# A recommender forward pass on one core: bottom parts placed ahead of the last gathered lots of the first chunk, and unread matmuls beside two waits

## The chip, the cores and the metric

The kernel runs on one core of a Trainium2 chip. The metric is the time of one execution on the device in microseconds; the median of several executions is given. The core has five engines with a queue of instructions each: TensorE (PE, matmuls and transposes), VectorE (DVE), ScalarE (ACT), GpSimd (POOL, here the gathers) and SyncE (SP, here the plain DMAs). Engines wait for one another on semaphores. What TensorE writes goes to PSUM, in banks of 512 float32 columns; everything else lies in SBUF, or in DRAM.

## What is computed

A batch of 512 samples has 13 dense numbers and 26 table indices each.

```python
def mlp(x, Ws, bs):
    for W, b in zip(Ws, bs):
        x = relu(x @ W + b)
    return x
bot_out = mlp(dense_x, [bw0, bw1, bw2], ...)              # 13 -> 512 -> 256 -> 128
gathered = stack([emb[t][sparse_x[:, t]] for t in range(26)], axis=1)
features = concatenate([bot_out[:, None, :], gathered], axis=1)   # 27 features of 128
Z = einsum('bnd,bmd->bnm', features, features)
interact = Z[:, LI, LJ]                                   # the 351 pairs i > j
x = concatenate([bot_out, interact], axis=1)              # 479
return mlp(x, [tw0, tw1, tw2, tw3, tw4], ...)             # 1024, 1024, 512, 256, 1
```

## The kernel before

The batch is cut into four chunks of 128 samples, a chunk into two halves of 64. The order on every engine is written out by hand; nothing reorders it. The chunks are software-pipelined: while TensorE does the top layers of chunk c, it also does the transposes and pair products of chunk c+1.

**Gathers.** GpSimd issues 26 indirect DMAs for each chunk, 13 for each half, in lots of 4, 4, 4 and 1. Each brings 128 rows of an embedding table. `pace` holds some of them back with waits on events of TensorE. In the fill (the gathers numbered up to 35), gather 31 waits for the second pair products of chunk 0 (`s_z` at 2). In chunk 0's stage, gather 37 waits until the first lot of chunk 1 is turned, and gather 39 for the end of layer 0's first half (`s_l[0]`).

**Features.** `turn_lot(c, h, j)` (L755) transposes a lot on TensorE into bank j of the tensor `feat`. `feature_lot` copies it from there into `featT`: ScalarE takes lots 0 and 2, VectorE lots 1 and 3. `dots_of(c, h)` waits for both copies and does the pair products of a half, 32 small matmuls in the program, 64 in the trace (L781). They are written into `feat` again. `dots_out` copies them out on ScalarE and VectorE into `dots`, SyncE writes them to a scratch in DRAM and reads them back with the pairs on the partitions, in three tiles (`pairs`). ScalarE rounds each tile to `xh` (L464), VectorE makes the rest `xl`.

**Top layers.** Layer 0 has two halves of 512 columns in the banks `acc0` and `acc1`, and three pair tiles. Each product is three matmuls (`product`, L799, L800 and L803): high part by high weight, high by low, low by high. The part of layer 0 that comes from the bottom output is worked out ahead: for chunk 0 into `acc0` and `acc1` directly, right behind the second pair products; for chunks 1 to 3 as six parts g = 0 to 5 (`bot_parts`), into the banks `turned0` (even g) and `turned1` (odd g) in turn. A part may be written when the copy of the part before it in the same bank is done; `bot_part_out` (L243) makes those copies, parts 0, 2, 4 and 5 on ScalarE (`s_prea`), 1 and 3 on VectorE (`s_pred`). They are read in chunks 1 to 3.

**Weights.** Each large weight arrives in pieces. ScalarE rounds a piece to its high part (L439), TensorE brings that into `acc0` and `acc1` by a product with the identity (`hi_back`, L823), and VectorE subtracts it from the raw weight (L595) to get the low part; `s_wl` counts these halves. Pieces 0 to 9 go that way; the last two of the group are subtracted without TensorE (L600).

"The regroup" is the stretch between the second pair products of chunk 0 and its layer 0, in which the pairs go through DRAM. Behind it SyncE issues the loads of w2, w3 and the top rows.

Of the kernel before, what the change touches and what calls it, by code (L numbers as in the profile page):

```python
# [23 lines left out]
P = 128  # L24
# [24 lines left out]
NB = 512  # L49
# [45 lines left out]
def after(eng, sem, count):  # L95

    if count > 0:
        eng.wait_ge(sem, count)


def rec_kernel(nc, x_turned, sparse, emb, bw, small, w0_bot, w0_pairs, w1, w2, w3_in, top_rows, scratch, out):
    with ExitStack() as ctx:
        def sb(name, shape, dt=F32, scope=ctx):
            return scope.enter_context(nc.sbuf_tensor(name, shape, dt))
# [53 lines left out]
        with ExitStack() as early:  # L158
            wbh = sb("wbh", [P, T0], F32R, early)
# [14 lines left out]
        def banks(name, n=1):  # L174
            return ctx.enter_context(nc.psum_tensor(name, [P, n * NB], F32))[:]

        acc = [banks("acc0"), banks("acc1")]
        turned = [banks("turned0"), banks("turned1")]
# [3 lines left out]
        def feat_bank(j):  # L182
            return feat[:, j * NB:(j + 1) * NB]

        def acc_of(c, half):
            return acc[half]
# [8 lines left out]
        s_wh, s_wb, s_wl, s_identr = map(sem, ("weight_hi", "weight_hi_in_psum", "weight_lo_halves", "ident_rounded"))  # L195
# [8 lines left out]
        s_bh, s_bl, s_pre, s_prea, s_pred = map(  # L204
            sem, ("bot_hi", "bot_lo", "bot_part_done", "bot_part_copied_act", "bot_part_copied_dve"))
# [24 lines left out]
        NEAR = UPPER - 2  # L230
# [7 lines left out]
        PARTS = 2 * (CHUNKS - 1)  # L238
        part_banks = [turned[g % 2] for g in range(PARTS)]

        def bot_part_out(eng, copy, g, done):
            eng.wait_ge(s_pre, g + 1)
            copy(bot_part[:, g // 2, g % 2 * NB:(g % 2 + 1) * NB], part_banks[g]).then_inc(done, 1)  # L243
# [7 lines left out]
        def lot_size(j):  # L251
            return min(LOT, GATHERS - LOT * j)

        def lot_out(h, j):
            n = PER_GATHER * lot_size(j)
            at = 1 + PER_GATHER * LOT * j
            return (featT[:, h, :, at:at + n].rearrange("d b n -> d n b"),
                    feat_bank(j)[:, 0:n * HALF].rearrange("d (n b) -> d n b", b=HALF))
# [172 lines left out]
        def _(act):  # L431
# [3 lines left out]
            def weight_hi(n):  # L435

                raw, hi, _ = pieces[n]
                act.wait_ge(s_piece[n], 16)
                nc.scalar.copy(hi, raw).then_inc(s_wh, 1)  # L439

            def feature_lot(c, h, j):

                act.wait_ge(s_ft, LOTS * (HALVES * c + h) + j + 1)
                nc.scalar.copy(*lot_out(h, j)).then_inc(s_fa, 1)  # L444

            def dots_out(c, h):

                after(act, s_scr0[h], 16 * c)
                after(act, s_scr1[h], 16 * c)
                act.wait_ge(s_z, HALVES * c + h + 1)  # L450
                nc.scalar.copy(*dot_quadrant(h, 0))
                nc.scalar.copy(*dot_quadrant(h, 1)).then_inc(s_za, 1)
# [62 lines left out]
            weight_hi(9)  # L515
            bot_part_out(act, nc.scalar.copy, 2, s_prea)
            weight_hi(NEAR)
            feature_lot(0, 1, 2)
            for g in range(PARTS - 2, PARTS):
                bot_part_out(act, nc.scalar.copy, g, s_prea)  # L520
            dots_out(0, 1)
            weight_hi(NEAR + 1)

# [230 lines left out]
        def _(pe):  # L754
            def turn_lot(c, h, j):  # L755

                half = HALVES * c + h
                pe.wait_ge(s_gather[LOTS * h + j], 16 * lot_size(j) * (c + 1))
                if j == 0:
                    after(pe, s_za, half)  # L760
                    after(pe, s_zd, half)
                for i in range(lot_size(j)):
                    ins = nc.tensor.transpose(feat_bank(j)[:, i * P:(i + 1) * P],  # L763
                                              rows[:, h * GATHERS + LOT * j + i, :], ident[:])
                ins.then_inc(s_ft, 1)

            def dots_of(c, h):

                half = HALVES * c + h
                pe.wait_ge(s_fa, 2 * half + 2)  # L770
                pe.wait_ge(s_fd, 2 * half + 2)
                pe.wait_ge(s_fb, half + 1)
                (sample_pairs if half < HALVES * CHUNKS - 1 else single_samples)(h)
# [23 lines left out]
            def product(dst, ah, al, wh, wl, first, end, lo_ready=None):  # L797

                nc.tensor.matmul(dst, ah, wh, start=first, stop=False)  # L799
                nc.tensor.matmul(dst, ah, wl, start=False, stop=False)  # L800
                if lo_ready is not None:
                    pe.wait_ge(*lo_ready)
                return nc.tensor.matmul(dst, al, wh, start=False, stop=end)  # L803

            def bot_times_w0(dst, c, half):

                at, cols = slice(c * P, (c + 1) * P), slice(half * NB, (half + 1) * NB)
                return product(dst[:], botTh[:, at], botTl[:, at], wbh[:, cols], wbl[:, cols], True, c > 0)

            def bot_parts(gs):  # L810
                for g in gs:
                    after(pe, s_pred if g % 2 else s_prea, g // 2)
                    bot_times_w0(part_banks[g], g // 2 + 1, g % 2).then_inc(s_pre, 1)

            def hi_back(n):

                if n == 0:
                    pe.wait_ge(s_identr, 1)
                    pe.wait_ge(s_h0, 2)
                pe.wait_ge(s_wh, n + 1)  # L820
                for x in range(2):
                    after(pe, s_wl, 2 * (n - 1) + x + 1)
                    nc.tensor.matmul(acc[x], ident_r, pieces[n][1][:, x * NB:(x + 1) * NB],  # L823
                                     start=True, stop=True).then_inc(s_wb, 1)
# [106 lines left out]
            for o in range(B0 // P):  # L931
                nc.tensor.matmul(bottom_banks[o][:], v0[:, o * P:(o + 1) * P], x0T[:], start=True,
                                 stop=True).then_inc(s_l0b, 1)
            pe.wait_ge(s_v[1], 16)
            for k in range(B0 // P):
                pe.wait_ge(s_h0, k + 1)
                for o in range(B1 // P):
                    ins = nc.tensor.matmul(turned[o][:], v1[:, k, o * P:(o + 1) * P], h0T[:, k, :],
                                           start=(k == 0), stop=(k == B0 // P - 1))
                    if k == B0 // P - 1:  # L940
                        ins.then_inc(s_l1b, 1)
                if k < 3:
                    hi_back(k)
                if k == 1:
                    pe.wait_ge(s_h0, B0 // P)
                    turn_lot(0, 0, 0)
            turn_lot(0, 0, 1)
            hi_back(3)
            pe.wait_ge(s_v[2], 16)
            for k in range(B1 // P):  # L950
                pe.wait_ge(s_h1, k + 1)
                ins = nc.tensor.matmul(turned[0][:], v2[:, k, :], h1T[:, k, :], start=(k == 0),
                                       stop=(k == B1 // P - 1))
            ins.then_inc(s_l2b, 1)
            hi_back(4)
            turn_lot(0, 0, 2)
            turn_lot(0, 0, 3)
# [10 lines left out]
            hi_back(8)  # L968
            bot_parts(range(2, 4))
            hi_back(9)  # L970
            turn_lot(0, 1, 2)
            turn_lot(0, 1, 3)
            bot_parts(range(4, 6))
            dots_of(0, 1)
            for half in range(2):
                pe.wait_ge(s_wl, 2 * (NEAR - 1) + half + 1)
                bot_times_w0(acc_of(0, half), 0, half)
            turn_lot(1, 0, 0)

            def chunk(c):  # L980
# [100 lines left out]
```

## Time and profile before

| | us |
|---|---|
| median of 3 runs | 182.41 |
| lowest and highest of them | 181.74, 182.44 |
| the profiled execution | 183.45 |
| its span, first to last instruction | 181.5 |
| TensorE busy in it | 166.4 |
| GpSimd busy in it | 100.7 |
| VectorE, ScalarE busy | 82.0, 66.6 |

The profiled execution lies above the three runs; the profile's times are on its own span, from 0 to 181.5 us. A row of the timeline gives start, length, engine, line, operation, what is written from what, and in brackets the idle time ahead of it with what ended it. Matmuls are pipelined: their lengths overlap, so the distance of two starts tells how fast they go. In the slices of the page each digit is the busy share of a fortieth of the span (4.54 us).

### The profile page before, as it was taken

To read this page: it belongs to the slowest core of one execution; us is meant where nothing else is said; L and a number is where in the kernel's file an instruction comes from. 1 tells how busy PE (TensorE), PEld (TensorE's weight loads), DVE (VectorE), ACT (ScalarE), POOL (GpSimd) and SP (SyncE) were. 2 spreads that over 40 slices of the span, in tenths; PEclk is the share of its full clock that TensorE was granted. 3 is DMA by queue.
4 is the path that set the end of the run, shared out by engine and by line. 5 is a ranking of instruction groups with operands and counts; after the bars stand their busy time and mean duration, and the time that the engine had idled before them with its cause. 6 is when DMAs were issued, how large, how long until landed. Compare 5 with 4: busy or idle time off the path is not lost.

```text
span 181.5 us, 3287 instructions
## 1 busy us (share of the span) xinstructions
PE 166.4 (92%) x1340; PEld 128.3 (71%) x1340; DVE 82.0 (45%) x177; ACT 66.6 (37%) x103; POOL 100.7 (55%) x112
## 2 busy tenths in 40 slices
PE   2999999779099999998999999999999999999993
PEld 1435557448066888797878889977887897788892
DVE  4204498924217557773443246253515625411422
ACT  0576858635031637432034253212514512110201
POOL 4777777776766777777777777777772000000000
PEclk9999999978958999999999999999999999999999
DMA  4989973322589924342222245322223120000000
GB/s 100 350 327 385 386 264 77 89 46 50 108 263 311 376 60 87 73 100 66 58 50 55 56 95 94 84 54 62 44 58 72 23 48 12 4 0 0 0 0 0
DMA packets 10122, 19.91 MB, mean 110 GB/s; under 512 B 5638, under 2 KB 5770, under 8 KB 9980
## 3 DMA queue, kind: packets, MB, share of 16 engines
q1 hardware_dynamic: 6636, 12.89, 22.1%
q0 software_dynamic: 3328, 6.82, 16.7%
q8 instruction: 10, 0.16, 0.4%
q14 instruction: 4, 0.03, 0.1%
q10 hardware_dynamic: 144, 0.00, 0.0%
HBM read 18.26 MB, written 1.44 MB: 109 GB/s over the span
## 4 chain that ended last, share of the span: by engine, by line
PE 42%; POOL 29%; DMA 12%; issue 12%; DVE 2%; SPq 1%; ACT 1%; POOLq 0%; DVEq 0%; ACTq 0%
POOL rows L420 29%; PE acc L799 10%; PE acc L803 9%; PE acc L800 9%; DMA rows<-in_emb,index 5%; PE feat L781 5%; DMA pairs<-pair_scratch 3%; DMA pair_scratch<-dots 3%; PE turned L875 2%; PE feat L763 2%; DMA index_raw<-in_sparse 1%; PE feat L793 1%; PE turned L889 1%; DVE dots L622 1%; DVE dots L621 1%
## 5 line engine op out<-in xcount | busy, mean ns | idle before, releaser
L420 POOL DMA_INDIRECT rows<-in_emb,index x104 | 99.5, 956 | 35.6 <-issue 30.3
L799 PE MATMUL acc<-w1h,y_split 128*128 128x512 f32 x64 | 27.4, 428 | 0.0
L803 PE MATMUL acc<-w1h,y_split 128*128 128x512 f32 x64 | 25.6, 400 | 0.0
L800 PE MATMUL acc<-w1l,y_split 128*128 128x512 f32 x64 | 25.2, 393 | 0.0
L457 ACT ACTIVATE y_split<-turned 128x512 fp32r<-128x512 f32 x16 | 9.7, 609 | 36.4 <-PE turned L875 36.4
L444 ACT COPY featT<-feat 128x512 f32<-128x512 f32 x16 | 17.5, 1093 | 12.9 <-PE feat L763 12.8
L651 DVE SCALAR_TENSOR_TENSOR y_split<-turned,y_split 128x512 fp32r<-128x512 f32 x16 | 11.1, 692 | 19.1 <-ACT y_split L457 19.0
L799 PE MATMUL acc<-w2h,y_split 128*128 128x256 f32 x64 | 18.9, 295 | 0.0
L763 PE MATMUL feat<-ident,rows 128*128 128x128 f32 x104 | 15.2, 275 | 3.2 <-DMA rows<-in_emb,index 3.2
L803 PE MATMUL acc<-w2h,y_split 128*128 128x256 f32 x64 | 18.0, 282 | 0.0
L800 PE MATMUL acc<-w2l,y_split 128*128 128x256 f32 x64 | 17.9, 280 | 0.0
L763 PEld LDWEIGHTS feat<-ident,rows 128*128 128x128 f32 x104 | 12.2, 140 | 7.2 <-DMA rows<-in_emb,index 4.6
L799 PE MATMUL acc<-w0h,xh 117*128 117x512 f32 (+1 forms) x24 | 12.2, 508 | 5.3 <-ACT xh L464 5.3
L781 PEld LDWEIGHTS feat<-featT 128*59 128x59 f32 x448 | 13.5, 141 | 2.9 <-issue 2.1
L607 DVE COPY featT<-feat 128x512 f32<-128x512 f32 (+1 forms) x16 | 11.8, 741 | 8.2 <-PE feat L763 8.2
L803 PEld LDWEIGHTS acc<-w1h,y_split 128*128 128x128 f32 x64 | 12.0, 188 | 4.3 <-DVE y_split L651 1.7
L781 PE MATMUL feat<-featT 128*59 128x54 f32 x448 | 14.4, 225 | 0.1
L799 PEld LDWEIGHTS acc<-w1h,y_split 128*128 128x128 f32 x64 | 12.2, 190 | 3.1 <-ACT y_split L457 1.4
L621 DVE COPY dots<-feat 27x416 f32<-27x416 f32 x8 | 4.7, 587 | 20.2 <-PE feat L781 19.5
L800 PEld LDWEIGHTS acc<-w1l,y_split 128*128 128x128 f32 x64 | 12.1, 189 | 1.7
L799 PEld LDWEIGHTS acc<-w2h,y_split 128*128 128x128 f32 x64 | 12.0, 188 | 0.2
L800 PEld LDWEIGHTS acc<-w2l,y_split 128*128 128x128 f32 x64 | 12.0, 188 | 0.0
(103 smaller groups left out, 253.9 us busy)
## 6 DMA issues: line engine op xcount, KB each, us to landing
w1r<-in_w SPq DMA_DIRECT2D x8, 512.0 KB, 15.1
w2r<-in_w SPq DMA_DIRECT2D x4, 512.0 KB, 6.1
rows<-in_emb,index POOLq DMA_INDIRECT x104, 3.1
w0r<-in_w_pairs SPq DMA_DIRECT2D x3, 512.0 KB, 8.8
top<-in_top_rows SPq DMA_DIRECT2D x1, 1024.0 KB, 11.6
pair_scratch<-dots SPq DMA_DIRECT2D x8, 104.0 KB, 2.4
pair_scratch<-dots SPq DMA_DIRECT2D x8, 71.5 KB
v<-in_bw SPq DMA_DIRECT2D x1, 512.0 KB, 3.7
```

The costliest lines, as they stand in the source:

```text
L420: pool.indirect_dma_start(rows[:, i, :], None, table, bass.IndirectOffsetOnAxis(ap=index[:, c, i:i + 1], axis=0)).then_inc(s_gather[LOTS * ...
L444: nc.scalar.copy(*lot_out(h, j)).then_inc(s_fa, 1)
L457: nc.scalar.activation(yh[:, half, :], turned[half][:], ACT.Relu).then_inc(s_yh[layer], 1)
L607: nc.vector.tensor_copy(*lot_out(h, j)).then_inc(s_fd, 1)
L621: nc.vector.tensor_copy(*dot_quadrant(h, 2))
L651: nc.vector.scalar_tensor_tensor(out=yl[:, half, :], in0=turned[half][:], scalar=0.0, in1=yh[:, half, :].bitcast(F32), op0=ALU.max, op1=AL ...
L763: ins = nc.tensor.transpose(feat_bank(j)[:, i * P:(i + 1) * P], rows[:, h * GATHERS + LOT * j + i, :], ident[:])
L781: ins = nc.tensor.matmul(feat[QUAD * q:QUAD * q + PAIR_COLS, at:at + 2 * FEATS].rearrange("n (s m) -> n s m", s=2), samples.rearrange("d s ...
L799: nc.tensor.matmul(dst, ah, wh, start=first, stop=False)
L800: nc.tensor.matmul(dst, ah, wl, start=False, stop=False)
L803: return nc.tensor.matmul(dst, al, wh, start=False, stop=end)
L875: ins = nc.tensor.transpose(turned[half][:, i * P:(i + 1) * P], y_evac[:, half, i * P:(i + 1) * P], ident[:])
```

## The change

On TensorE, bottom parts 4 and 5 are put ahead of the transposes of the last two lots of chunk 0 instead of behind them. Ahead of the second pair products come three matmuls of 512 columns into `acc0` whose result nobody reads, behind a wait on the weight difference that last read that bank. Between the bottom products of chunk 0 and the transposes of chunk 1's first lot come eleven such matmuls into `turned0`, behind a wait for three copies of parts on ScalarE. On ScalarE the copy of part 4 goes ahead of the copy of lot 2.

```diff
@@ scalar
             weight_hi(NEAR)
+            bot_part_out(act, nc.scalar.copy, PARTS - 2, s_prea)
             feature_lot(0, 1, 2)
-            for g in range(PARTS - 2, PARTS):
-                bot_part_out(act, nc.scalar.copy, g, s_prea)
+            bot_part_out(act, nc.scalar.copy, PARTS - 1, s_prea)
             dots_out(0, 1)
             weight_hi(NEAR + 1)
@@ tensor
+            def keep_going(bank, times):
+                for _ in range(times):
+                    nc.tensor.matmul(bank[:], wbh[:, 0:P], wbh[:, 0:NB], start=True, stop=True)
@@ tensor
             hi_back(9)
+            bot_parts(range(4, 6))
             turn_lot(0, 1, 2)
             turn_lot(0, 1, 3)
-            bot_parts(range(4, 6))
+            pe.wait_ge(s_wl, 2 * (NEAR - 1) + 1)
+            keep_going(acc[0], 3)
             dots_of(0, 1)
             for half in range(2):
                 pe.wait_ge(s_wl, 2 * (NEAR - 1) + half + 1)
                 bot_times_w0(acc_of(0, half), 0, half)
+            pe.wait_ge(s_prea, PARTS // 2)
+            keep_going(turned[0], 11)
             turn_lot(1, 0, 0)
```

How it stands on the engines. TensorE around the last two lots of chunk 0, before: the transposes (L763), then part 4 (`turned0`) and part 5 (`turned1`), then the pair products (L781).

```order
50 L823 MATMUL acc1<-w1h,xl 128x512
51 L763 MATMUL feat<-ident,rows 128x128 x5
52 L799 MATMUL turned0<-wbh,botTh 128x512
53 L800 MATMUL turned0<-wbl,botTh 128x512
54 L803 MATMUL turned0<-wbh,botTl 128x512
55 L799 MATMUL turned1<-wbh,botTh 128x512
56 L800 MATMUL turned1<-wbl,botTh 128x512
57 L803 MATMUL turned1<-wbh,botTl 128x512
58 L781 MATMUL feat<-featT 59x54 x32
```

The same place of TensorE in the changed kernel (L829 is the line that was L823, L819 the unread matmul).

```order
50 L829 MATMUL acc1<-w1h,xl 128x512
51 L799 MATMUL turned0<-wbh,botTh 128x512
52 L800 MATMUL turned0<-wbl,botTh 128x512
53 L803 MATMUL turned0<-wbh,botTl 128x512
54 L799 MATMUL turned1<-wbh,botTh 128x512
55 L800 MATMUL turned1<-wbl,botTh 128x512
56 L803 MATMUL turned1<-wbh,botTl 128x512
57 L763 MATMUL feat<-ident,rows 128x128 x5
58 L819 MATMUL acc0<-wbh 128x512 x3
59 L781 MATMUL feat<-featT 59x54 x32
```

The two parts stand ahead of the five transposes, and three unread matmuls between these and the products.

ScalarE at the same place, the difference (L444 is the copy of lot 2).

```order
 L439 CAST w1h<-w1r 128x1024
+L243 COPY bot_part<-turned0 128x512
 L444 COPY featT<-feat 128x8x64
-L243 COPY bot_part<-turned0 128x512
 L243 COPY bot_part<-turned1 128x512
 L451 COPY dots<-feat 27x26x16
```

The copy of part 4 has moved ahead of the lot copy; that of part 5 has stayed.

TensorE in the regroup of the changed kernel, between the last bottom product of chunk 0 and layer 0 (before, L763 stands directly behind L803).

```order
65 L803 MATMUL acc1<-wbh,botTl 128x512
66 L819 MATMUL turned0<-wbh 128x512 x11
67 L763 MATMUL feat<-ident,rows 128x128 x4
68 L799 MATMUL acc0<-w0h,xh 128x512
69 L800 MATMUL acc0<-w0l,xh 128x512
```

Eleven unread matmuls stand ahead of the transposes of chunk 1's first lot. The orders of VectorE, GpSimd and SyncE are the same.

## Rows read from the trace of the kernel before

**Rows 1.** The page: span, TensorE's slices, and the clock row.

```profile
span 181.5 us, 3287 instructions
...
PE   2999999779099999998999999999999999999993
...
PEclk9999999978958999999999999999999999999999
```

**Rows 2.** The chain that ended last: start us, us, what was worked on.

```profile
39.90 0.43 PE turned L800
...
70.77 2.93 DMA rows<-in_emb,index
...
74.31 0.23 PE acc L800
...
112.23 0.95 POOL rows L420
```

**Rows 3.** Timeline of TensorE's matmuls: start us, us, engine, line, operation, count [idle before].

```profile
26.56 1.94 PE L781 MATMUL feat<-featT 128*59 128x54 f32 x64
...
32.36 0.66 PE L763 MATMUL feat<-ident,rows 128*128 128x128 f32 x4 [0.68 <-DMA rows<-in_emb,index]
...
34.90 0.92 PE L823 MATMUL acc<-w1h,xl 128*128 128x512 f32 x2
37.34 0.66 PE L763 MATMUL feat<-ident,rows 128*128 128x128 f32 x4 [1.52 <-DMA rows<-in_emb,index]
38.29 0.33 PE L763 MATMUL feat<-ident,rows 128*128 128x128 f32 x1 [0.29 <-DMA rows<-in_emb,index]
...
40.68 2.72 PE L781 MATMUL feat<-featT 128*59 128x54 f32 x64
...
44.84 0.60 PE L763 MATMUL feat<-ident,rows 128*128 128x128 f32 x4
49.76 0.79 PE L799 MATMUL acc<-w0h,xh 117*128 117x512 f32 x1 [4.32 <-ACT xh L464]
...
52.88 0.79 PE L799 MATMUL acc<-w0h,xh 118*128 118x512 f32 x1 [0.20 <-ACT xh L464]
...
73.75 0.33 PE L763 MATMUL feat<-ident,rows 128*128 128x128 f32 x1 [0.43 <-DMA rows<-in_emb,index]
```

**Rows 4.** Timeline of ScalarE, 34 to 50 us.

```profile
34.42 0.59 ACT L243 COPY bot_part<-turned 128x512 f32<-128x512 f32 x1 [1.39 <-PE turned L803]
...
38.03 1.07 ACT L444 COPY featT<-feat 128x512 f32<-128x512 f32 x1 [2.08 <-PE feat L763]
...
49.41 0.30 ACT L464 CAST xh<-pairs 118x128 fp32r<-118x128 f32 x1 [3.88 <-DMA pairs<-pair_scratch]
```

**Rows 5.** Timeline of VectorE, 35 to 44 us.

```profile
35.18 0.68 DVE L243 COPY bot_part<-turned 128x512 f32<-128x512 f32 x1
35.78 1.27 DVE L595 TENSOR_TENSOR w1l<-w1r,acc 128x512 fp32r<-128x512 f32 x2
...
43.45 0.59 DVE L621 COPY dots<-feat 27x416 f32<-27x416 f32 x1 [4.40 <-PE feat L781]
```

**Rows 6.** Timeline of GpSimd: the gathers around the two waits.

```profile
43.69 0.94 POOL L420 DMA_INDIRECT rows<-in_emb,index  x1 [1.04 <-PE feat L781]
...
52.47 0.95 POOL L420 DMA_INDIRECT rows<-in_emb,index  x1 [0.30 <-issue]
55.33 1.08 POOL L420 DMA_INDIRECT rows<-in_emb,index  x1 [1.91 <-PE acc L803]
```

**Rows 7.** Windows of 1 us: stretch, length, busy us by engine, granted clock, DMA share, GB/s.

```profile
39.00:40.00 1.00, 1.00 (x4) 0.81 (x3) 0.06 (x1) 0.60 (x2) 0.78 (x1) 0.50 0.27 62
42.00:43.00 1.00, 1.00 (x36) 1.00 (x34) 0.00 (x0) 0.00 (x0) 0.65 (x1) 0.80 0.33 66
...
49.00:50.00 1.00, 0.24 (x1) 0.24 (x2) 0.26 (x1) 0.30 (x1) 0.70 (x2) 0.62 0.40 96
...
56.00:57.00 1.00, 1.00 (x8) 0.83 (x7) 0.59 (x2) 0.00 (x0) 0.70 (x2) 0.97 1.11 352
```

## Prediction

> **What bounds the kernel now.** I read the page's own slices first, then the chain of work that ended last, then the timelines of the five engines from 34 to 60 us, and last the windows that give TensorE's granted clock.
>
> The page shows TensorE busy in nines almost everywhere; the thin places after the fill are slices 8 to 13, and the clock row dips in the same ones [rows 1]. So a gain there counts only if the work behind it can start earlier too.
>
> The chain says what that work is. Over the last gathered rows, the bottom parts (in which a matmul of 0.43 us stands on it), the second pair products, the copies and the scratch round trip it comes to layer 0, and from the end of layer 0's first half it goes back to GpSimd, whose gathers carry it from 55.33 to the landing of chunk 1's last row block at 73.70 (70.77 and 2.93); TensorE carries it on to 112.23, where gathers take it again [rows 2, 6]. There is one chain with two runners: TensorE and the gather engine. TensorE reached the last block of chunk 1 only 0.43 us before it landed [rows 3].
>
> In TensorE's timeline the reader is to see four things. After the weight products with the identity end at 35.82 it idles until 37.34, and again 0.29 before 38.29 [rows 3]. Then it runs the six matmuls of parts 4 and 5 before the products, which start at 40.68 although the ScalarE copy of lot 2, their last input, was over at 39.10 [rows 3, 4]. Then the products take 2.72 us where the same 64 took 1.94 in the first half [rows 3]. Last, after the regroup's transposes it idles 4.32 us until layer 0 at 49.76 [rows 3].
>
> The clock explains the lengths. It is low (1.2 GHz) by 39.0, since the stretch from 39 to 40 has 0.50 throughout; it is full (2.4 GHz) again at about 42.4 (0.80 over 42 to 43), low at about 49.2 (0.62 over 49 to 50), and full from about 56.1 (0.97 over 56 to 57) [rows 7]. A 512-column matmul starts every 0.43 us at the low level and every 0.23 at the full one [rows 2].
>
> **Part 1: parts 4 and 5 ahead of the last two lots.** They need copies of parts 2 and 3, done at 35.01 on ScalarE and 35.86 on VectorE [rows 4, 5]. Part 4 can follow at once at 35.65, part 5 at about 36.3: six matmuls at 0.23 are 1.4 us and end near 37.1, in the idle stretch before 37.34. So they cost nothing there; at the low level they would take 2.6 and hold the last lots up by about 0.9. The clock is full there, so I take nothing. On ScalarE the copy of part 4 now stands ahead of the copy of lot 2, and behind that one stands lot 2's semaphore for the products. Part 4 is finished near 36.5, a copy is 0.59, so it is over by 37.1 and the lot copy still starts at 38.03 [rows 4]. The copy of part 5 stays behind the lot copy and ends near 39.7, before the products are over. VectorE, SyncE and GpSimd keep their order.
>
> The products' start moves from 40.68 to 39.15, 0.05 behind the lot copy (39.10): **1.53 us**.
>
> **Part 2: 3 unread matmuls ahead of the products.** They wait for the first half of the weight difference that VectorE began at 35.78 and ended (both halves) by 37.05 [rows 5], so for nothing. The last transpose starts at 38.29; three at 0.23 fill 38.4 to 39.1, when TensorE would wait for the lot copy. Cost nothing at the full level, and up to 0.5 at the low one. With the 1.5 us hole and this one filled, what went ahead of the fall at 39.0 is gone, and the products run at the full level: 1.94 and not 2.72, which is **0.78 us**. Sum: the products end at 41.1, not 43.4, **2.3 us** earlier.
>
> **Part 3: what hangs on the products.** Copies out, scratch write and read are fixed steps: 43.45 on VectorE to 49.41 (first pair tile on ScalarE) is 5.96 [rows 4, 5]. So xh comes at 47.1, layer 0 at 47.45 and not 49.76, its third tile's matmuls at 50.58 and not 52.88 [rows 3].
>
> **Part 4: 11 unread matmuls in the regroup.** They wait for three ScalarE copies of parts (0, 2 and 4), long done. The six bottom products for chunk 0 run 41.1 to 42.5, then 11 at 0.23, 2.5 us, to about 45.1, then the four transposes, to 45.7. Layer 0 is due at 47.45, so they cost nothing: slack 1.7 us. They leave two idle stretches, 45.7 to 47.45 and (its six first matmuls take 1.4) 48.9 to 50.58. Moved behind them are those transposes (44.84 before, 45.1 now), whose copy on ScalarE comes only behind the third pair tile; the gather that waits for them would start at 50.5. Nothing is late.
>
> Is the clock still full for layer 0? Unseen in this trace; I bound it. If full throughout: before, from 52.88 to 56.1 TensorE worked at half rate, 1.6 us lost, all of it regained. If low until the very same moment 56.1: 50.58 to 56.1 at half rate loses 2.8, that is 1.2 more than before. The idle that went ahead of the first fall was 1.5 plus 0.3 us with transposes between [rows 3], and 1.75 plus 1.7 is no less, so I lean to a low stretch that remains. TensorE's own gain at 56 us is then between 1.1 (2.3 less 1.2) and 3.9 (2.3 plus 1.6).
>
> **Part 5: the gather engine caps it.** One gather waits for the products: it starts at 43.69 with the one before done at 42.65; with the usual 0.30 it starts at 42.95 [rows 6], 0.74 earlier. The seven up to the one at 52.47 follow at the same pace: the last of them starts at 51.73 and is done at 52.68. The next waits for layer 0's first half, 2.45 behind the third tile's first matmul (52.88 to 55.33), so 53.03 with 50.58; GpSimd itself is free at 52.98. So 55.33 becomes 53.0: **2.3 us**, and by no clock more. The twelve gathers behind it, to the one that leaves at 70.77, are 1.28 apart on average and wait for none of the events that TensorE would now reach later than they do, so the last block lands at 71.4. TensorE, with a gain of 1.1 to 3.9 and its 0.43 of idle, is there 1.5 to 4.3 earlier. What counts is the smaller: **1.5 to 2.35**. Behind it all moves alike: the same round trip for chunk 1, the gathers at 112.23 released by TensorE.
>
> Sum against the profiled execution: 183.45 (span 181.5 and 1.95 around it), less 1.5 to 2.35, is 181.1 to 181.95. It stands 1.04 over the median of 182.41, and I carry the difference over: 180.06 to 180.9. The three runs differ by 0.70, so before itself does not always lose the same to the clock; that, too, speaks for less than the cap. I take 1.9: **180.5**.
>
> **A rule that speaks against it.** The rows: the clock fell at 39.0 after a stretch in which near half of TensorE's busy time was transposes [rows 3, 7]. The Trainium skill, TensorE: Matmul & The Clock Gate, Part 4: PE-mode transpose, says that transposes don't count as TensorE activity the way matmuls do. By that the two lots at 37.34 and 38.29 stay a hole for the clock in spite of parts and fillers around them; by the row alone it is the idle that matters, and that is gone. The trace agrees with either.
>
> **The rivals.**
> Rival 1, the clock falls near 39 all the same: for it, 1.0 us of transposes and 0.5 of idle remain there; against it, a 0.68 us wait at 32.36, between dense work, was followed by no fall [rows 3, 7]. The 2.72 us of before held 1.7 at the low level and 1.0 at the full; with 1.94 for all at the full one, all at the low one would be 3.6. Started at 39.3 and low until 42.4 they end at 42.7, 0.7 earlier. Time 181.7.
> Rival 2, the round trip gives it back: it now runs beside other gathers, with w2's loads queued right behind it. If the 5.96 us become 8, only 0.3 is left: 182.1. Against it: the loads shift along, and the gathers beside it are as many as before.
> Rival 3, slower: the low level lasts from 39.0 through the regroup. Fillers to 39.8, products to 43.4 (3.6 us, the end of before), six matmuls to 46.0, 11 fillers of 0.43 to 50.7, transposes to 51.6, layer 0's first six to 54.2; the third tile began at 52.88 before. That is 1.3 later: 183.7. It decides where the regroup's fillers outlast the round trip: 1.7 us of slack against 2.2 of extra filler time alone. Against it: in before the level rose at 42.4 under dense work.
> That fillers are not issued is excluded: the order has both groups, 3 and 11.
>
> **How the numbers follow.** Forecast 0.76 (179.9 to 181.0), rival 1 0.11, rival 2 0.09, rival 3 0.04. The range for 8 in 10 runs from 179.8, a little under the cap, to 181.8, which takes in rival 1. A measurement here tells 0.5%, 0.9 us, from no change: faster 0.78 (the forecast and the good edge of rival 1, 0.02), same 0.17, slower 0.05.
>
> **What would show it.** In the changed profile: parts 4 and 5 at 35.6 to 37.1; products near 39.2, 1.9 long, with the clock full from 38 to 43; the 11 at 42.5 to 45.1; layer 0 at about 47.5; the gather of 55.33 at 53.0 with about 0.3 idle before it; TensorE waiting longer than 0.43 for the last block of chunk 1 near 71.4. It is wrong if the products take over 2.5 us (rival 1), if 5.96 us from the products to xh grows (rival 2), if layer 0 finds xh waiting (rival 3), or if a wait further on takes the lead, such as the w2 and w3 loads.

## The result, and the profile after

| | before | changed |
|---|---|---|
| median of 20 runs, us | 182.7 | 181.2 |
| lowest, us | 180.56 | 180.47 |
| profiled execution, us | 183.45 | 181.54 |
| its span, us | 181.5 | 179.6 |
| mean granted clock in it | 0.972 | 0.991 |

The ratio of the changed kernel to before is 0.9933, with an interval from 0.9912 to 0.9954: faster by 0.5 to 0.9 per cent, about 1.2 us. Every ratio here is taken over the fast runs alone, without those more than 1.5 per cent above the fastest of their kernel, and every median over all runs. The forecast was 180.5 and a gain of 1.9. The two profiled executions differ by exactly that, 1.9; the medians by 1.5.

The page of the changed kernel, against [rows 1]: the clock dips of slices 9 to 13 are gone, and one stands further on.

```profile
span 179.6 us, 3315 instructions
...
PE   1999999899599994999999999989999999999993
...
PEclk9999999999999999799999999999999999999999
```

TensorE's timeline of the changed kernel, against [rows 3] (start us, us, engine, line, operation, count, idle before):

```profile
36.41 0.39 PE L799 MATMUL turned<-wbh,botTh 128*128 128x512 f32 x1
...
37.79 0.60 PE L763 MATMUL feat<-ident,rows 128*128 128x128 f32 x4
38.61 0.33 PE L763 MATMUL feat<-ident,rows 128*128 128x128 f32 x1 [0.22 <-DMA rows<-in_emb,index]
38.69 0.95 PE L819 MATMUL acc<-wbh 128*128 128x512 f32 x3
39.57 1.94 PE L781 MATMUL feat<-featT 128*59 128x54 f32 x64
...
42.94 2.66 PE L819 MATMUL turned<-wbh 128*128 128x512 f32 x11
45.43 0.60 PE L763 MATMUL feat<-ident,rows 128*128 128x128 f32 x4
47.97 0.50 PE L799 MATMUL acc<-w0h,xh 117*128 117x512 f32 x1 [1.94 <-ACT xh L464]
...
50.01 0.40 PE L799 MATMUL acc<-w0h,xh 118*128 118x512 f32 x1
...
70.37 0.65 PE L763 MATMUL feat<-ident,rows 128*128 128x128 f32 x4 [1.81 <-DMA rows<-in_emb,index]
71.69 0.48 PE L763 MATMUL feat<-ident,rows 128*128 128x128 f32 x1 [0.67 <-DMA rows<-in_emb,index]
...
74.63 1.95 PE L781 MATMUL feat<-featT 128*59 128x54 f32 x64
```

Parts 4 and 5 lie ahead of the lots, the products start right behind the three unread matmuls and take 1.94 us, layer 0 starts 1.8 us earlier than at 49.76. And then TensorE waits 1.81 and 0.67 us for the last two lots of chunk 1, where it had waited 0.43.

GpSimd's timeline of the changed kernel, against [rows 6]:

```profile
43.28 1.09 POOL L420 DMA_INDIRECT rows<-in_emb,index  x1 [0.30 <-issue]
...
52.16 0.94 POOL L420 DMA_INDIRECT rows<-in_emb,index  x1 [0.30 <-issue]
53.41 0.94 POOL L420 DMA_INDIRECT rows<-in_emb,index  x1 [0.30 <-issue]
```

The gather that had waited for the products left at 43.28 instead of 43.69, the one that had waited 1.91 us for layer 0 left at 53.41 instead of 55.33, and neither waited for anything but GpSimd itself: 0.30 is the gap between any two gathers.

The windows of the changed kernel, against [rows 7] (stretch, length, busy us of five engines, granted clock, DMA share, GB/s):

```profile
39.00:40.00 1.00, 1.00 (x19) 0.62 (x18) 0.36 (x1) 0.92 (x2) 0.69 (x2) 1.00 0.19 49
...
54.00:55.00 1.00, 1.00 (x5) 0.76 (x5) 0.65 (x2) 0.00 (x0) 0.69 (x2) 1.00 0.94 348
...
70.00:71.00 1.00, 0.63 (x4) 0.42 (x4) 0.25 (x1) 0.00 (x0) 0.97 (x1) 1.00 0.43 95
71.00:72.00 1.00, 0.33 (x3) 0.31 (x3) 0.00 (x0) 0.94 (x2) 0.69 (x2) 0.56 0.43 86
72.00:73.00 1.00, 1.00 (x4) 0.81 (x4) 0.80 (x2) 0.51 (x2) 0.70 (x2) 0.50 0.07 16
```

In this execution the clock is full through both places where it was low before. It falls at about 71.1 instead, in the new wait for the gathers. There it costs something: between the last lot and the second products of chunk 1 lie six matmuls. Before, they filled 73.83 to 75.40; now 71.82 to 74.63. So 2.06 us of gain at the lot (73.75 to 71.69) are 0.77 at these products (75.40 to 74.63) and 1.39 at chunk 1's layer 0 (84.62 to 83.23; TensorE waited 0.59 there before and does not now).

From there to the end of the gathers the gain stays near 1.2: it is 1.17 at the last group of eight transposes of chunk 3 (137.57 to 136.40). What makes it 1.9 at the end comes after them, at the last block gathered of all:

```profile
136.24 4.17 DMA rows<-in_emb,index
...
140.46 0.33 PE L763 MATMUL feat<-ident,rows 128*128 128x128 f32 x1 [0.28 <-DMA rows<-in_emb,index]
...
142.11 1.49 PE L793 MATMUL feat<-featT 128*27 128x27 f32 x128
```

These are rows of the kernel before, the first of the chain and the others of TensorE's timeline: the block took 4.17 us from issue to landing, where the median of the 104 gathers is 3.1, and TensorE waited for it. In the changed kernel TensorE did not wait there, and the same last products started at 140.45 and took 1.27. The change touches nothing at that place, and the trace of the order alone has such a wait (0.48) and the same 1.49, that of the old order with 11 neither. So about 0.7 of the 1.9 us between the two profiled executions looks like a difference of executions and not of kernels; the rest agrees with the 1.2 of the ratio.

### The profile page after: what moved, and what is told of

Its sections match the earlier page's. It is cut to its first block, busy times and chain, and to the rows that moved or that the text cites. A ratio compares the mean times of both kernels' runs of the same rounds, so it can differ in the third digit from the quotient of the medians.

```text
span 179.6 us, 3315 instructions
## 1 busy us (share of the span) xinstructions
PE 167.0 (93%) x1354; PEld 128.6 (72%) x1354; DVE 82.2 (46%) x177; ACT 66.3 (37%) x103; POOL 100.7 (56%) x112
## 4 chain that ended last, share of the span: by engine, by line
PE 71%; DMA 10%; POOL 8%; issue 4%; SPq 2%; DVE 2%; ACT 2%; POOLq 0%; DVEq 0%; ACTq 0%
PE acc L799 14%; PE acc L803 13%; PE acc L800 12%; POOL rows L420 8%; PE feat L781 6%; PE turned L944 5%; PE feat L763 5%; DMA rows<-in_emb,index 3%; PE turned L881 3%; DMA pairs<-pair_scratch 3%; DMA pair_scratch<-dots 3%; PE acc L829 2%; PE acc L938 2%; PE feat L938 2%; DMA v<-in_bw 1%
## 5 line engine op out<-in xcount | busy, mean ns | idle before, releaser
L799 PE MATMUL acc<-w1h,y_split 128*128 128x512 f32 x64 | 27.9, 436 | 0.0
L803 PE MATMUL acc<-w1h,y_split 128*128 128x512 f32 x64 | 26.1, 407 | 0.0
L444 ACT COPY featT<-feat 128x512 f32<-128x512 f32 x16 | 17.6, 1097 | 14.4 <-PE feat L763 14.3
L803 PE MATMUL acc<-w2h,y_split 128*128 128x256 f32 x64 | 18.0, 281 | 0.0
L763 PE MATMUL feat<-ident,rows 128*128 128x128 f32 x104 | 15.3, 277 | 2.7 <-DMA rows<-in_emb,index 2.7
L763 PEld LDWEIGHTS feat<-ident,rows 128*128 128x128 f32 x104 | 12.3, 141 | 6.6 <-DMA rows<-in_emb,index 3.9
L803 PEld LDWEIGHTS acc<-w1h,y_split 128*128 128x128 f32 x64 | 12.3, 192 | 4.4 <-DVE y_split L651 1.7
L781 PEld LDWEIGHTS feat<-featT 128*59 128x59 f32 x448 | 12.7, 134 | 2.9 <-issue 1.7
L799 PEld LDWEIGHTS acc<-w1h,y_split 128*128 128x128 f32 x64 | 12.5, 195 | 3.1 <-ACT y_split L457 1.4
L781 PE MATMUL feat<-featT 128*59 128x54 f32 x448 | 13.6, 219 | 0.1
L799 PE MATMUL acc<-w0h,xh 117*128 117x512 f32 (+1 forms) x24 | 10.9, 455 | 2.7 <-ACT xh L464 2.7
L799 PEld LDWEIGHTS acc<-w2h,y_split 128*128 128x128 f32 x64 | 12.0, 188 | 0.2
L803 PEld LDWEIGHTS acc<-w2h,y_split 128*128 128x128 f32 x64 | 12.0, 187 | 0.2 <-DVE y_split L651 0.2
```

Of the source, the lines that this page charges most:

```text
L781: ins = nc.tensor.matmul(feat[QUAD * q:QUAD * q + PAIR_COLS, at:at + 2 * FEATS].rearrange("n (s m) -> n s m", s=2), samples.rearrange("d s ...
```

## The experiments

Theory 1: the earlier products bring the whole scratch round trip forward, and the gather engine caps what that can give. Theory 2: the unread matmuls, through the clock, are what counts.

The twelve kernels ran in three jobs, each on one chip with the kernel before beside them. The jobs fell on two kinds of chip, which nobody chose: in the second job the median of before was 183.3 us, in the first and the third 214.2 and 213.9. A ratio is only good inside its job. In job 2 the order alone has 7 runs and the changed kernel with a gather less 6; the others have 12.

| job | kernel | median us | ratio to before | interval |
|---|---|---|---|---|
| 1, chip 7 | order alone | 213.89 | 1.0002 | 0.9973 to 1.0032 |
| | order and 3 | 213.22 | 0.9953 | 0.9918 to 0.9987 |
| | order and 11 | 213.51 | 0.9979 | 0.9947 to 1.0012 |
| | old order and 11 | 214.29 | 0.9962 | 0.9922 to 1.0001 |
| 2, chip 3 | order alone | 181.72 | 0.9902 | 0.9867 to 0.9938 |
| | old order and 11 | 182.44 | 0.9973 | 0.9936 to 1.0009 |
| | changed, a gather less | 180.63 | 0.9828 | 0.9785 to 0.9871 |
| | before, the same gather less | 182.94 | 0.9997 | 0.9965 to 1.0029 |
| 3, chip 15 | the changed kernel | 213.72 | 0.9987 | 0.9951 to 1.0023 |
| | order alone | 213.98 | 0.9992 | 0.9959 to 1.0025 |
| | order and 3 | 213.57 | 0.9985 | 0.9946 to 1.0024 |
| | changed, 18 for 11 | 214.49 | 1.0018 | 0.9991 to 1.0044 |

### The order alone

The changed kernel without both groups of unread matmuls:

```diff
-            pe.wait_ge(s_wl, 2 * (NEAR - 1) + 1)
-            keep_going(acc[0], 3)
...
-            pe.wait_ge(s_prea, PARTS // 2)
-            keep_going(turned[0], 11)
```

> Only the new order: parts 4 and 5 ahead of the last two lots, the ScalarE copy of part 4 ahead of the lot copy, no unread matmuls. Theory 1 (the round trip and the gather cap): the products start at about 39.3 and end 1.5 to 2.3 us earlier, the gather that waited for layer 0 leaves at about 53 or soon after, and the low clock in layer 0 is absorbed by the wait of TensorE for the last lots of chunk 1; the gain is nearly that of the whole change: ratio 0.993 to 0.996. Theory 2 (the unread matmuls and their clock are what counts): the products still run at the low level or layer 0 does, and the ratio is 0.998 to 1.000.

> Once more only the new order, no unread matmuls, since the first job ran on a chip on which every version takes 213 us. Where the time of before is near 182 us: Theory 1 (round trip earlier, gather engine as the cap) 0.993 to 0.996, with the gather that waited for layer 0 leaving at about 51 to 53 and a low clock in layer 0. Theory 2 (the unread matmuls bring it): 0.998 to 1.000.

On chip 3 it measured 0.9902, more than Theory 1 said; on the other two chips 1.0002 and 0.9992, which is no gain. On chip 3 the order alone is as good as the whole change was against its own before (0.9933); the intervals overlap. Its timeline of TensorE in job 2:

```profile
39.89 0.33 PE L763 MATMUL feat<-ident,rows 128*128 128x128 f32 x1 [0.38 <-DMA rows<-in_emb,index]
40.74 1.94 PE L781 MATMUL feat<-featT 128*59 128x54 f32 x64 [0.52 <-ACT featT L444]
...
49.14 0.79 PE L799 MATMUL acc<-w0h,xh 117*128 117x512 f32 x1 [3.13 <-ACT xh L464]
...
72.22 1.11 PE L763 MATMUL feat<-ident,rows 128*128 128x128 f32 x5 [0.44 <-DMA rows<-in_emb,index]
...
74.66 1.94 PE L781 MATMUL feat<-featT 128*59 128x54 f32 x64
```

The gather that waits for layer 0, which had left at 55.33 and was expected at about 51 to 53:

```profile
54.67 0.95 POOL L420 DMA_INDIRECT rows<-in_emb,index  x1 [0.30 <-issue]
```

Its windows in layer 0, and in the wait for the last lots:

```profile
53.00:54.00 1.00, 1.00 (x3) 0.71 (x3) 0.61 (x2) 0.00 (x0) 0.69 (x2) 0.50 1.15 393
...
70.00:75.00 5.00, 4.44 (x36) 3.24 (x36) 4.28 (x11) 3.51 (x4) 3.94 (x4) 1.00 0.40 87
```

The products take 1.94 us without the three unread matmuls. Layer 0 does run at the low level, as the eleven were meant to avoid. This execution was late from its start (its products begin at 40.74, 1.2 us behind those of the changed kernel), and so was GpSimd: the gather left at 54.67, but with no more than the usual 0.30 idle, so it is GpSimd itself that sets it. TensorE waits 0.44 and not 2.48 us for the last lots, keeps its full clock there, and begins the second products of chunk 1 at 74.66; the changed kernel did at 74.63. In these two traces the low stretch is paid for in one place or in the other. That speaks for Theory 1, and against Theory 2 as far as it says that the unread matmuls are needed.

It does not take the clock out of the account. Twelve of the 21 runs of before that the ratio takes in job 2 have a mean clock of 0.970 to 0.972, as the profiled one with its low stretch near 39; none of the seven runs of the order alone is under 0.976. At 0.976 to 0.981 the order alone has a median of 181.85 (five runs), before 182.16 (nine), and before with a gather less 182.9 (eight). How much of the 0.9902 is the earlier round trip, and how much the low stretch that comes no more, these runs do not separate.

### The old order with the 11 unread matmuls

```diff
             bot_parts(range(4, 6))
             dots_of(0, 1)
...
+            pe.wait_ge(s_prea, PARTS // 2)
+            keep_going(turned[0], 11)
             turn_lot(1, 0, 0)
```

> The order of before with the 11 unread matmuls in the regroup alone. Theory 1: the products end when they did (43.4), layer 0 starts at 49.8 at the full clock, the gather that waits for its first half leaves about 0.6 us earlier, so 0.997 to 1.000. Theory 2: the full clock in layer 0 gives 1 to 1.6 us: 0.992 to 0.995.

> Once more the order of before with the 11 unread matmuls in the regroup alone. Theory 1: the products end as in before, the gather that waits for layer 0 leaves up to 0.6 us earlier: 0.997 to 1.000. Theory 2: 0.992 to 0.995.

0.9973 on chip 3, within what Theory 1 said; but the interval, 0.9936 to 1.0009, takes in 1 and also half of what Theory 2 said, so the time decides nothing. On chip 7 it was 0.9962, a little better than Theory 1 said. The trace from chip 3 shows something else as well. Up to the products this is the order of before, with the same idle stretches, and yet:

```profile
37.88 0.66 PE L763 MATMUL feat<-ident,rows 128*128 128x128 f32 x4 [1.22 <-DMA rows<-in_emb,index]
39.23 0.33 PE L763 MATMUL feat<-ident,rows 128*128 128x128 f32 x1 [0.69 <-DMA rows<-in_emb,index]
...
40.89 1.94 PE L781 MATMUL feat<-featT 128*59 128x54 f32 x64
```

The products took 1.94 us, and the windows from 38 to 43 us have a clock of 1.00. The fall of the clock that cost [rows 3] its 2.72 us does not come in each execution of that order. And further on, against [rows 6]:

```profile
49.57 0.50 PE L799 MATMUL acc<-w0h,xh 117*128 117x512 f32 x1 [2.22 <-ACT xh L464]
...
53.56 1.08 POOL L420 DMA_INDIRECT rows<-in_emb,index  x1 [0.38 <-issue]
...
73.69 1.94 PE L781 MATMUL feat<-featT 128*59 128x54 f32 x64
```

Theory 1 gave this gather at most 0.6 us; it left 1.77 earlier than before, only 0.08 behind the moment at which GpSimd was free for it, though layer 0 began 1.6 us later than in the changed kernel. The clock was full up to 50.9 and low from there to 54.3, 3.4 us; in before the low stretch of layer 0 is 6.8 us long. So in this execution the old order with a clock full for longer reached the cap of the gather engine as well. The cap is real, but the new order is not the only way to it: the two theories do not exclude one another as they were set up. The gains of the two changes then need not add up.

### One gather less

In both kernels the single gather of the last lot of chunk 1's first half is left out, and its lot is turned from chunk 0's rows; so that part of the output is not computed. TensorE's waits for that lot are lowered to match; the diff shows the gather's side alone.

```diff
                     pace(c * HALVES * GATHERS + i)
+                    if (c, h, j) == (1, 0, LOTS - 1):
+                        continue
```

> The changed kernel with one gather left out: the single one that makes up the last lot of chunk 1's first half; the rows of chunk 0 are turned in its place. It takes 1.25 us off the gather engine ahead of the last lots of chunk 1. Theory 1 (in the changed kernel the gather engine is the bound up to there, TensorE waits 1.8 and 0.7 us for its last lots): 1.0 to 1.3 us faster than the changed kernel, so about 0.986 to 0.989 of before. Theory 2 (the gather engine is no cap, TensorE itself is): no faster than the changed kernel, 0.993.

> The kernel before with the same gather left out. There GpSimd waits 1.9 us for layer 0 ahead of chunk 1's gathers anyway, and TensorE has only 0.43 us of waiting for the last lots. The gather left out stands ahead of that wait, so Theory 1 expects nothing to 0.3 us: 0.998 to 1.000. Theory 2 (gathers are a steady bound everywhere, in before too): 0.993.

In the changed kernel it brings the ratio to 0.9828, in before to 0.9997. A gather costs GpSimd 1.25 us. Before had that to spare, since GpSimd waits for layer 0 just behind it; the trace of that run shows the wait grown from 1.91 to 2.36 (GpSimd had waited for TensorE in the fill, and was free 1.0 us earlier than in before, not 1.25; the end of layer 0's first half also came 0.5 earlier):

```profile
54.81 1.08 POOL L422 DMA_INDIRECT rows<-in_emb,index  x1 [2.36 <-PE acc L806]
```

With the change the gather left out shows in the time. The run stands 1.1 us below the order alone of the same job (180.63 and 181.72); the changed kernel itself was not in that job, so the size is less sure than the sign. Theory 1 said 0.986 to 0.989, so 0.9828 is more than a gather's time explains. The trace says where it may come from (L422, L766 and L784 are the gather, the transposes and the products there):

```profile
52.65 1.08 POOL L422 DMA_INDIRECT rows<-in_emb,index  x1 [0.69 <-issue]
...
70.50 0.66 PE L766 MATMUL feat<-ident,rows 128*128 128x128 f32 x4 [0.41 <-DMA rows<-in_emb,index]
71.34 0.33 PE L766 MATMUL feat<-ident,rows 128*128 128x128 f32 x1 [0.18 <-DMA rows<-in_emb,index]
...
72.98 1.94 PE L784 MATMUL feat<-featT 128*59 128x54 f32 x64
```

The gather behind layer 0 left 0.76 earlier than in the changed kernel, TensorE waited 0.59 for the last lots and not 2.48, and the clock did not fall there. The last lot was turned only 0.35 earlier (71.34 and 71.69), but the products began 1.65 earlier (72.98 and 74.63), since the six matmuls between ran at the full level. Earlier, in layer 0, the clock did fall in this execution, from 49.7 to 53.1, in spite of the eleven unread matmuls.

So the gather engine bounds the changed kernel and not the one before, as Theory 1 has it, and this pair is the clearest split between the two theories; but part of what a gather less gives comes through the clock.

### Order and 3, order and 11, the changed kernel again, 18 for 11

```diff
-            keep_going(turned[0], 11)
+            keep_going(turned[0], 18)
```

Order and 3 and order and 11 leave out one group each, the order alone both.

> The new order and the 3 unread matmuls ahead of the products, none in the regroup. Theory 1: as the whole change, 0.993 to 0.995, with a low clock from 48 or 49 us that costs TensorE 1 to 2 us in layer 0, hidden behind the gather engine. Theory 2: half of the gain is missing, 0.997 or more.

> The new order and the 11 unread matmuls in the regroup, not the 3 ahead of the products. Theory 1: 0.993 to 0.995; the 3 only matter where the clock would fall before the products. Theory 2: in between the order alone and the whole change.

> The changed kernel once more, so that it stands in one job with the order alone. Theory 1 (the order brings the gain, the gather engine caps it) expects it within 0.3 per cent of the order alone, both at 0.990 to 0.995. Theory 2 (the unread matmuls add the clock) expects it 0.5 per cent or more below the order alone.

> The order alone, in the same job as the changed kernel. Theory 1: 0.990 to 0.995, within 0.3 per cent of the changed kernel. Theory 2: 0.996 or more.

> The order and the 3 unread matmuls ahead of the products, none in the regroup. Theory 1: as the order alone, 0.990 to 0.995; the products take 1.94 us with or without the 3. Theory 2: half way from the order alone to the changed kernel.

> The changed kernel with 18 unread matmuls in the regroup and not 11, 1.6 us more of them; TensorE idled 1.94 us there in the changed kernel, so they end at about 47.6, still ahead of layer 0 at 47.97. Theory 1: no change against the changed kernel in time (within 0.2 per cent); the fall of the clock in layer 0 becomes rarer, which the gather engine hides. Theory 2: 0.3 to 0.8 per cent faster than the changed kernel, since the clock stays full through layer 0. A slower result would mean that the fillers reach into layer 0.

All of these fell on the chips of 214 us, so they cannot rank the unread matmuls for the other kind. What they show is that the whole change is worth nothing there that can be told from no change: 0.9987, 0.9992, 0.9985, and 1.0018 with 18. Order and 3 had 0.9953 on chip 7 and 0.9985 on chip 15; only the first interval leaves 1 out. The 18 stand 0.3 per cent above the changed kernel, outside both expectations; the two intervals overlap. Neither theory expected all this: the order alone came where Theory 2 put it, but adding the unread matmuls did not bring what Theory 2 said either.

Why the change does nothing there can be seen, if not explained. ScalarE in the changed kernel on chip 15:

```profile
44.31 0.59 ACT L243 COPY bot_part<-turned 128x512 f32<-128x512 f32 x1 [2.12 <-PE turned L803]
47.90 1.01 ACT L444 COPY featT<-feat 128x512 f32<-128x512 f32 x1 [3.00 <-remote]
```

And TensorE:

```profile
44.20 0.33 PE L763 MATMUL feat<-ident,rows 128*128 128x128 f32 x1 [0.35 <-issue]
44.29 0.95 PE L819 MATMUL acc<-wbh 128*128 128x512 f32 x3
48.96 3.45 PE L781 MATMUL feat<-featT 128*59 128x54 f32 x64 [3.73 <-ACT featT L444]
```

The lots are turned by 44.5, but the copy that waits for them starts at 47.90, and so does VectorE's of the other lot at 47.93. Then the products run at the low level. In the old order (with the 11) on chip 7 the products start earlier and come in pieces; the chain of that run:

```profile
45.44 0.93 PE feat L781 x27
46.38 0.68 issue
...
47.98 1.20 issue
49.18 0.25 PE feat L781
49.43 0.48 issue
49.91 1.93 PE feat L781 x33
```

They end at 51.84; in the new order on chip 7 they start at 48.07, take 3.45 and end at 51.5. In either order the products end at about the same moment, and the time by which they could start earlier is lost. Such idle stretches stand ahead of, or in, most groups of pair products on these chips. The profile names nothing that TensorE waits for in the pieces (`issue`); no run here tests what it is, and it stays open.

## Why the prediction was right, and where it was off

The time lay in the range and the direction held. The gain was 1.2 us, with 0.8 to 1.6 in its interval, and 1.9 was forecast. That the two profiled executions differ by just 1.9 is luck: 0.7 of it arose at the last gathered block. Two steps made the forecast too large: 0.78 us for the clock in the products, taken as lost in every execution of before, and "behind it all moves alike", which put the new wait for the gathers at nothing.

- **Part 1, the order.** Right. Parts 4 and 5 ended by about 37.8 in time for the lots, ScalarE copied part 4 ahead of the lot, and the products started at 39.57, where 39.2 was expected; TensorE was 0.8 later in its fill in this execution already. The order alone measured 0.9902.
- **Part 2, the three unread matmuls and 0.78 us for the clock in the products.** This term was mis-sized. The 1.94 us came, but not through the three: the order alone has it too. And 0.78 us is only lost in those executions of before in which the clock falls near 39; two other traces with the old order up to there, the old order with 11 and before with a gather less, had 1.94. Of the 21 runs of before that the ratio takes in job 2, the twelve with a mean clock of 0.970 to 0.972 have a median of 183.5; the nine with 0.978 to 0.981 have 182.2, and by their mean clock one low stretch fewer. I took one execution's low stretches for the kernel's. The spread of 0.70 in the three runs was seen, but it was used to choose inside the bounds, not to take the term down.
- **Part 3, the round trip.** Right: 41.56 on VectorE to 47.62 on ScalarE is 6.06, against 5.96. The third tile came sooner than its place in before said, and layer 0's third product started at 50.01, not 50.58.
- **Part 4, the eleven.** They cost nothing in the regroup, as said (1.94 us of idle left, 1.75 expected). Whether the clock stays full in layer 0 was the unknown. It did, and the lean towards a low stretch was wrong for this execution. With the same eleven it was right for two others: the clock fell at 50.9 (old order with 11) and at 49.7 (changed, a gather less), for 3.4 us each, where the traces without the eleven (before, order alone, before with a gather less) have 6.8 us. What was overlooked is the next step: an earlier TensorE waits longer for the gathers, and the clock can fall there. The six matmuls behind the last lot then took 2.81 us and not 1.57, so 1.2 of the 2.06 us were lost again. Of the 17 runs of the changed kernel that the ratio takes, 14 have a mean clock of 0.988 to 0.991, the profiled one's; that is about one low stretch of 3.4 us in each, here or in layer 0. The one run with 1.000 took 180.72, against a median of 181.0 for these 14.
- **Part 5, the cap.** Right up to the last block of chunk 1: 53.41 against 53.0, with 0.30 idle and not 1.91; the last block at 71.69 against 71.4; 2.48 us of waiting for the last two lots. The gather left out agrees in sign in both kernels. "Behind it all moves alike" is what failed: the 2.06 us at that block were 0.77 at the products behind it.
- **The rule on transposes.** The clock did not fall at 39 in the changed kernel, with 0.9 us of transposes in that stretch, nor with the order alone, nor in two traces of the old order, with 1.0 us of them and 1.5 to 1.9 us of idle. By the Trainium skill, TensorE: Matmul & The Clock Gate, Part 4: PE-mode transpose, they do not count like matmuls; these rows neither need nor refute it.
- **The rivals.** Rivals 1 and 3 did not come in the profiled execution: the clock is 1.00 from 38 to 70. Rival 2 did not either, with 6.06 us. On chip 15 the products of the changed kernel did run at the low level, 3.45 us long, as in rival 1, but they also started late. None of the rivals, nor the forecast, had a chip on which the change is worth nothing.

Open: what the unread matmuls are worth on the faster kind of chip, within one job, was not measured. The order alone (0.9902) and the whole (0.9933) come from two jobs. Not separated either is how much of the gain of the order is the earlier round trip and how much the low stretch near 39 that it ends.

## What to carry to other kernels

When a wait is shortened, follow the gain to the next engine that paces the same chain, and work out when that engine is free with no wait at all: here a gather every 1.25 us capped a gain of TensorE of up to 3.9 us at about 2. Then look at what the new wait does: keeping TensorE busy in one wait moved the low stretch of the clock to the next one in the trace of the changed kernel, and 1.2 us went with it. When two changes both bring the chain to the same cap, do not add their gains. And a low stretch in one profiled execution is a sample: look at the mean clock of several runs before it goes into a sum.

## What was not expected of the hardware

- The same program, the kernel before, took 181.7 to 185.4 us on one chip and 211.8 to 216.1 on two others. On those, ScalarE, VectorE and GpSimd started together over 3 us after the transposes that they waited for: in the changed kernel on chip 15 at 47.90, 47.93 and 48.17, with the last transpose over at 44.53; in the order alone on chip 7 at 47.01, 47.04 and 47.28, with 43.50.
- The first load that TensorE waits for landed at different times in nearly equal programs: its first matmul started at 3.47 to 3.60 us in three traces of the faster kind and at 4.54 to 4.92 in three others. In all but the trace of before, GpSimd's paced gathers waited about 0.8 us at one to three places of the fill.
